# Twelve key tiles' product and denominators, and the order of GpSimd's first zero rows

## The chip, the cores and the metric

The kernel runs on one core of one Trainium2 chip. The core has five engines that run their own instruction streams and meet at semaphores: TensorE (PE in the profile; its weight loads are PEld), VectorE (DVE), ScalarE (ACT), GpSimd (POOL) and SyncE (SP), which issues the transfers. The metric is the device time in microseconds. The kernel before took 3111.95, 3116.89 and 3116.89 us in three runs; the median is 3116.89.

## The reference

Two layers of attention with a feed-forward block behind each, on x of 2 x 1024 x 1024 in fp32, each block on a layer norm of x and added to it. The attention has 32 query heads of 32 dimensions in 8 groups that share a key and value head; rotary positions; a causal softmax.

```python
q = (x @ wq).reshape(bsz, seq_len, N_HEADS, HEAD_DIM)
k = (x @ wk).reshape(bsz, seq_len, N_KV_HEADS, HEAD_DIM)
v = (x @ wv).reshape(bsz, seq_len, N_KV_HEADS, HEAD_DIM)
q = _apply_rope(q, cos, sin)
k = _apply_rope(k, cos, sin)
...
scores = jnp.einsum('bqhd,bkhd->bhqk', q, k) / np.float32(np.sqrt(HEAD_DIM))
scores = scores + mask
attn = jax.nn.softmax(scores.astype(jnp.float32), axis=-1).astype(q.dtype)
out = jnp.einsum('bhqk,bkhd->bqhd', attn, v).reshape(bsz, seq_len, N_HEADS * HEAD_DIM)
return out @ wo
```

The blocks behind are a mixing layer over four streams and a mixture of low-rank experts; the change touches neither.

## The kernel before

`build` runs attention of layer 0, the mixing layer, attention of layer 1, the output projection and the experts, one after the other. Only `attention` matters here.

**Numbers in halves.** x and the weights are split into a high part, rounded, and a low rest (`xT_hi`, `xT_lo`, `w_hi`, `w_lo`), and each projection piece is three matmuls (hi by hi, lo by hi, hi by lo; L759). Queries and keys are stacked in the same way, three parts of 32 dimensions in 96 partitions (`qst`, `kst`). Partitions 96 to 127 carry the row maximum: -1 in the keys' last row, the maximum in the queries' last row, zeros in the 31 rows between.

**Groups.** A group is one key head with its four query heads, in one batch; 2 layers x 2 batches x 8 groups make 32. For a group, the scores are computed transposed, keys in partitions, in twelve units: e counts the pairs of a query half (qc) and a key tile (ki). A unit has two steps of scores (`("ST", e, half)`, L827), which ScalarE turns into `prob` by an exponential (L560), and the steps `("PV", e, 0)`, the product with V into `ppv`, and `("PV", e, 1)`, the denominators, a product with ones, into `pden` (both L847: eight matmuls in a profile row, or two times four, each with weights 32 columns wide). Below they are called V.e and D.e. The four heads are of 512, 384, 256 or 128 columns by the unit's place at the causal edge.

**What is woven between.** The exponential wants the row maximum beforehand. So while group g is multiplied, the scores of group g+1 are computed once more in the plain direction only for their maxima: 38 uses `("S", k)` (L780) into `psh`, two banks in turn, and VectorE takes the maxima out (L647 with the causal edge, L650 without). S.k can start when VectorE has released the bank of S.(k-2) (the semaphore `sh_free`). Also into `psh` go the two projections of a later group's queries, `("P", c, i)` (eight pieces each of three matmuls); VectorE's rotation of P.0 (L635, L636, the second a shuffle) releases its bank, which is that of S.1. `("MT", 0)` transposes the maxima once VectorE has gathered them (L656); they go out to memory and back into the last row of the stacks.

**The order** is written out by `iteration()`: a dictionary `after` gives for each step what stands behind it; S uses are dealt out over the units 1 to 9 in proportion to columns. There are four orders: `body` (24 groups, all of it), `body6` (`proj=False`, 4 groups), `ahead7` (2 groups, without S and P.0, P.1, with the next batch's x tiles instead) and `body7` (2 groups, nothing woven in). Every engine walks the same list and does its own part of each step.

**The head of an attention.** VectorE takes statistics of each of the eight x tiles (`statistics`, L610), GpSimd the power -1/2 of the variance (`reciprocal_deviation`, L420), VectorE normalises (L619), TensorE transposes (L771), and projects. On GpSimd the eight powers stand first, with the first weights' low part (`w_lo`, L425) behind the sixth; then come the constant rows of the two stacks (L492, L494, L496); then the turn-over (the rotary sine part, `turn_over`, L432 and L434) of the first projection and the low part of the second weights.

Of the kernel before, what the change touches and what calls it, by code (L numbers as in the profile page):

```python
# [14 lines left out]
F32 = mybir.dt.float32  # L15
# [6 lines left out]
P = 128  # L22
B, S, D = 2, 1024, 1024
T = B * S
NT = T // P
ST_ = S // P
# [3 lines left out]
GH = 4  # L30
# [46 lines left out]
def columns(step):  # L77

    what, e, _ = step
    n = BANK - unit_offset(e)  # L80
    return 2 * max(n, BANK // 2) if what == "ST" else 4 * n


def iteration(full_s=True, proj=True, ahead=False):

    steps = [[("ST", e + 1, 0), ("ST", e + 1, 1), ("PV", e, 0), ("PV", e, 1)] for e in range(NU)]
    steps[-1] = steps[-1][2:]  # L90
    after = {step: [] for unit in steps for step in unit}
    first = []
    if proj:
        quarter = lambda c, i: [("P", c, k) for k in range(i * PIECES // 4, (i + 1) * PIECES // 4)]
        first = quarter(0, 0)
        for i, step in enumerate(steps[0][:3]):
            after[step] += quarter(0, i + 1)
        after[steps[2][1]] += [("HI", 0)]
        after[steps[3][1]] += [("LO", 0)]
        after[steps[2][0]] += [("WL", 0)]  # L100
        after[steps[4][0]] += [("WS", 0)]
        after[steps[5][0]] += [("RS", 0)]
        after[steps[10][1]] += quarter(1, 0)
        after[steps[10][2]] += quarter(1, 1) + [("RK", 0)]
        after[steps[10][3]] += quarter(1, 2) + quarter(1, 3)
    if full_s:
        window = [step for unit in steps[1:10] for step in unit]
        total, done, k = sum(map(columns, window)), 0, 0
        for step in window:
            done += columns(step)  # L110
            while k < len(USES) and k * total < done * len(USES) - total // 2:
                after[step] += [("S", k)]
                k += 1
        assert k == len(USES)
        after[steps[10][1]] += [("MT", 0)]
    after[steps[10][1]] += [("NORM", 0)]
    if ahead:


        for i in range(ST_):  # L120
            after[steps[i][0]] += [("XS", i)]
            after[steps[i][2]] += [("XN", i)]
            after[steps[i + 2][1]] += [("XT", i)]
            after[steps[i + 2][2]] += [("XC", i)] + [("XL", i + NX_AHEAD)] * (i + NX_AHEAD < ST_)
        first = [("XL", i) for i in range(NX_AHEAD)]
        for i in range(PIECES):
            after[steps[10][i * 3 // PIECES]] += [("P", "next", i)]
    order = [("ST", 0, 0), ("ST", 0, 1)] + ([("HI", 1), ("LO", 1), ("RS", 1)] if full_s else []) + first
    for unit in steps:
        for step in unit:  # L130
            order += [step] + after[step]
    return order + [("NORM", 1)]
# [57 lines left out]
def attention(nc, sem, layer, x_in, wqkv, cos_in, sin_in, swap, oT_d):  # L190
# [21 lines left out]
    ZT0, W0, SH0, R0, E0, PV0, AC0, N0, ST0, DMA0 = 4, 2, 1, 4, 2, 2, 2, 1, 2, 16  # L212

    pro, body, body6, body7 = prologue(), iteration(), iteration(proj=False), iteration(False, False)
    ahead7 = iteration(False, False, True)
    plan_pro, U_PRO = bank_plan(pro, spare=(2, 3, 4, 5))
    plan = {id(order): bank_plan(order)[0] for order in (body, body6, body7, ahead7)}
# [4 lines left out]
    with ExitStack() as ctx:  # L222
        def sb(name, shape, dt=F32):
            return ctx.enter_context(nc.sbuf_tensor(f"a{layer}_{name}", shape, dt))
# [17 lines left out]
        qst = [sb(f"qst{i}", [P, GH, S], F32R) for i in range(2)]  # L242
# [173 lines left out]
        def _(pool):  # L416
            def reciprocal_deviation(tile, k):

                pool.wait_ge(s["stats"], tile + 1)
                pool.tensor_tensor(mv[k % 2][:, 3:4], mv[k % 2][:, 2:3], nhalf[:, :], ALU.pow).then_inc(s["pow"], 1)  # L420

            def w_lo(n, par):
                pool.wait_ge(s["w_hi"], n + 1)
                pool.sem_inc(s["pool_turn"], 1)
                pool.tensor_tensor(w[par][1][:, :, :], wraw[par][:, :, :], w[par][0][:, :, :].bitcast(F32),  # L425
                                   ALU.subtract).then_inc(s["w_ready"], 1)
# [56 lines left out]
            pool.drain().then_inc(s["const"], 1)  # L483
            pool.drain().then_inc(s["w_ready"], W0)
            pool.drain().then_inc(s["roped"], R0)
            for k in range(ST_):
                reciprocal_deviation(k, k)
                if k == 5:
                    w_lo(0, 0)
            pool.drain()  # L490
            for i in range(2):
                pool.memset(kst[i][96:P, :].bitcast(F32), -1.0)  # L492
                pool.drain()
                pool.memset(kst[i][96:P - 1, :].bitcast(F32), 0.0)  # L494
                pool.drain()
                pool.memset(qst[i][96:P - 1, :, :].bitcast(F32), 0.0)  # L496
                pool.drain()
            pool.drain().then_inc(s["padded"], 1)

# [248 lines left out]
        def _(pe):  # L748
            def project(n, u, where, par, c, piece):

                _, at, prev = where
                if piece == 0:
                    pe.wait_ge(s["w_ready"], W0 + n + 1)
                    pe.wait_ge(s["sh_free"], SH0 + u + prev + 1)
                passes = [(k, a, x) for k in range(KC) for a, x in ((0, 0), (0, 1), (1, 0))]
                step = len(passes) // PIECES
                for i in range(piece * step, (piece + 1) * step):
                    k, a, x = passes[i]
                    mm = pe.matmul(bank(at), w[par][a][:, k, :], xT[x][:, k, c * BANK:(c + 1) * BANK],  # L759
                                   start=(i == 0), stop=(i == len(passes) - 1))  # L760
                if piece == PIECES - 1:
                    mm.then_inc(s["sh_ready"], 1)
# [12 lines left out]
            def row_scores(u, where, par, k):  # L775
                _, at, prev = where
                qt, kc, n, heads, _ = USES[k]
                pe.wait_ge(s["sh_free"], SH0 + u + prev + 1)
                for i, h in enumerate(heads):
                    mm = pe.matmul(psh[:, at, i * n:(i + 1) * n], qst[par][0:P - 1, h, qt * P:(qt + 1) * P],  # L780
                                   kst[par][0:P - 1, kc * BANK:kc * BANK + n], start=True, stop=True,
                                   skip_group_check=True)
                mm.then_inc(s["sh_ready"], 1)

            def transpose_max(n, u, where):
                _, at, prev = where
                pe.wait_ge(s["mx_ready"], n + 1)
                pe.wait_ge(s["sh_free"], SH0 + u + prev + 1)
                pe.transpose(psh[0:GH * ST_, at, 0:P], mx[:, 0, :], ident[:, :]).then_inc(s["sh_ready"], 1)
# [1131 lines left out]
```

## Time and profile before

| | us |
|---|---|
| runs | 3111.95, 3116.89, 3116.89 |
| profiled execution | 3121.41 |
| its span, first to last instruction | 3119.7 |
| TensorE busy in it | 2780.3 (89%) |
| VectorE busy | 1933.4 (62%) |
| ScalarE busy | 1001.4 (32%) |
| GpSimd busy | 715.2 (23%) |

The profile is one execution. Its clock column (PEclk) is the share of full speed that TensorE was granted; the mean over the span is 0.945. Three views are used: windows, which give each engine's busy time in a stretch; the timeline, which gives start, length and number of instructions of a row; and at a row's end, in brackets, how long the engine had been idle before and what released it. Matmuls overlap, so the time of one is read from start to next start, not from its length.

### The profile page before, as it was taken

The numbers are of one execution on the slowest core, as the hardware profiler recorded it, in microseconds if no ns is written. First come the engines' busy times: TensorE is split into PE (matmuls) and PEld (weight loads), VectorE is DVE, ScalarE is ACT, GpSimd is POOL, SyncE is SP. The second block draws the span as 40 slices with busy tenths as digits, with TensorE's granted clock in tenths as the row PEclk, the third lists the DMA queues.
The fourth block names the chain that finished last, engine by engine and source line by source line (L and its number), as shares of the span: only waits on it lengthen the run. The fifth ranks groups of instructions, "written<-read, shape, count | busy, mean of one in ns | idle before, by whom it ended". The sixth has DMA issues, their size and how long they took to land. (4 is left out here: it accounts for less than half of the span.)

```text
span 3119.7 us, 49191 instructions
## 1 busy us (share of the span) xinstructions
PE 2780.3 (89%) x15824; PEld 1788.4 (57%) x15824; DVE 1933.4 (62%) x4357; ACT 1001.4 (32%) x1549; POOL 715.2 (23%) x693
## 2 busy tenths in 40 slices
PE   7899998999999799652859999989999996997999
PEld 5545554655554488652646455436555542885887
DVE  4577777557777433588765677775677774324543
ACT  2143435134343411352521443433244344101000
POOL 6223231433231000000044323214223220001111
PEclk8999999999999899765979999989999998998999
DMA  3323222323131422000123323223323221443111
GB/s 139 102 64 89 70 72 72 113 73 97 56 102 30 140 81 67 0 0 0 81 115 105 101 63 89 69 64 110 94 63 97 58 77 73 158 135 148 68 67 41
DMA packets 121063, 252.84 MB, mean 81 GB/s; under 512 B 12720, under 2 KB 39728, under 8 KB 120880
## 3 DMA queue, kind: packets, MB, share of 16 engines
q1 hardware_dynamic: 120912, 251.03, 25.5%
q8 instruction: 69, 1.13, 0.2%
q14 instruction: 82, 0.67, 0.1%
HBM read 166.57 MB, written 84.41 MB: 80 GB/s over the span
## 5 line engine op out<-in xcount | busy, mean ns | idle before, releaser
L560 ACT ACTIVATE a_prob<-a_pst 128x1024 f32<-128x1024 f32 (+3 forms) x768 | 593.0, 814 | 726.2 <-PE a_pst L827 724.7
L647 DVE CUSTOM_DVE_ANT_0 a_psh<-a_psh,a_edge 128x128 f32<-128x128 f32 (+3 forms) x1024 | 487.6, 514 | 218.5 <-PE a_psh L780 208.1
L780 PE MATMUL a_psh<-a_kst,a_qst 127*128 127x512 f32 (+3 forms) x1536 | 511.7, 394 | 29.3 <-issue 12.0
L780 PEld LDWEIGHTS a_psh<-a_kst,a_qst 127*128 127x128 f32 x1536 | 255.9, 189 | 455.4 <-DVE a_mx L647 199.3
L827 PE MATMUL a_pst<-a_qst,a_kst 128*128 128x512 f32 (+2 forms) x1536 | 398.8, 361 | 28.9 <-ACT a_prob L560 11.0
L650 DVE TENSOR_REDUCE a_mx<-a_psh 128x1 f32<-128x512 f32 x512 | 343.6, 689 | 71.1 <-PE a_psh L780 65.1
L847 PE MATMUL a_ppv<-a_prob,a_vg 128*32 128x512 f32 (+3 forms) x3072 | 335.0, 508 | 15.6 <-POOL a_prob L464 10.6
L464 POOL TENSOR_SCALAR_AFFINE_SELECT a_prob<-a_prob 128x512 f32<-128x512 f32 x256 | 171.9, 672 | 759.4 <-ACT a_prob L560 758.2
L827 PEld LDWEIGHTS a_pst<-a_qst,a_kst 128*128 128x128 f32 x1536 | 267.1, 192 | 128.4 <-issue 56.2
L847 PE MATMUL a_pden<-a_prob,a_ones 128*32 128x512 f32 (+3 forms) x3072 | 332.0, 504 | 0.0
L691 DVE RECIPROCAL a_dens<-a_dens 128x512 f32<-128x512 f32 x64 | 214.6, 3353 | 75.6 <-ACT a_dens L568 66.4
L432 POOL TENSOR_TENSOR a_swp<-a_swp,a_sin 128x512 f32<-128x512 f32 x80 | 103.2, 1290 | 330.3 <-DVE a_swp L636 329.6
L759 PE MATMUL a_psh<-a_xT_hi,a_w_hi 128*128 128x512 f32 x416 | 174.4, 419 | 2.3 <-issue 1.6
L1411 PE MATMUL h_pout<-h_w,h_o 128*128 128x512 f32 x720 | 167.7, 392 | 0.8 <-DVE h_x L1288 0.8
L759 PE MATMUL a_psh<-a_xT_lo,a_w_hi 128*128 128x512 f32 x416 | 165.2, 397 | 0.0
L759 PE MATMUL a_psh<-a_xT_hi,a_w_lo 128*128 128x512 f32 x416 | 164.9, 396 | 0.0
L425 POOL TENSOR_TENSOR a_w_lo<-a_wraw,a_w_hi 128x1024 fp32r<-128x1024 f32 x50 | 119.2, 2383 | 178.9 <-ACT a_w_hi L536 163.0
L759 PE MATMUL a_pst<-a_xT_hi,a_w_hi 128*128 128x512 f32 x352 | 141.7, 403 | 13.2 <-POOL a_w_lo L425 9.0
L1411 PEld LDWEIGHTS h_pout<-h_w,h_o 128*128 128x128 f32 x720 | 134.1, 188 | 28.8 <-DMA h_wb<-in_w_branch 1.2
L647 DVE DVE_READ_ACCUMULATOR2_ANT a_mx<- 128x1 f32 x1024 | 145.0, 142 | 0.0
L759 PE MATMUL a_pst<-a_xT_lo,a_w_hi 128*128 128x512 f32 x352 | 139.5, 396 | 0.0
L759 PE MATMUL a_pst<-a_xT_hi,a_w_lo 128*128 128x512 f32 x352 | 139.1, 395 | 0.0
(217 smaller groups left out, 3958.8 us busy)
## 6 DMA issues: line engine op xcount, KB each, us to landing
a_qst<-q SPq DMA_DIRECT2D x192, 256.0 KB, 4.5
a_wraw<-in_wqkv SPq DMA_DIRECT2D x52, 512.0 KB, 5.7
q<-a_stg_hi SPq DMA_DIRECT2D x64, 256.0 KB, 2.6
q<-a_stg_lo SPq DMA_DIRECT2D x64, 256.0 KB, 2.8
oT<-a_oT SPq DMA_DIRECT2D x64, 256.0 KB, 2.5
a_kst<-kT SPq DMA_DIRECT2D x96, 128.0 KB, 3.0
h_oraw<-oT SPq DMA_DIRECT2D x16, 512.0 KB, 4.1
h_x<-in_x SPq DMA_DIRECT2D x16, 512.0 KB, 4.7
```

The source lines that it names most:

```text
L425: pool.tensor_tensor(w[par][1][:, :, :], wraw[par][:, :, :], w[par][0][:, :, :].bitcast(F32), ALU.subtract).then_inc(s["w_ready"], 1)
L432: pool.tensor_tensor(swp[c][:, :], swp[c][:, :], sin[:, c * BANK:(c + 1) * BANK], ALU.mult)
L464: pool.affine_select(out=blk, in_=blk, compare_op=ALU.is_ge, fill=0.0, base=0, pattern=[[0, GH], [1, P]], channel_multiplier=-1)\
L560: act.activation(prob[k % 2][:, 2 * half:2 * half + 2, off:], pst[:, half, :, off:], ACT.Exp, scale=scale).then_inc(s["exp_done"], 1)
L647: part = dve.tensor_tensor_reduce(scores, scores, edge[:, BANK - n:], 1.0, 2 * MASKED, ALU.add, ALU.max, mx_hq[kc][:, h, qt:qt + 1])
L650: part = dve.tensor_reduce(mx_hq[kc][:, heads[0]:heads[0] + m, qt], psh[:, at, 0:m * n].rearrange("p (m n) -> p m n", n=n), AX.X, ALU.max)
L691: dve.reciprocal(dens[:, :], dens[:, :])
L759: mm = pe.matmul(bank(at), w[par][a][:, k, :], xT[x][:, k, c * BANK:(c + 1) * BANK], start=(i == 0), stop=(i == len(passes) - 1))
L780: mm = pe.matmul(psh[:, at, i * n:(i + 1) * n], qst[par][0:P - 1, h, qt * P:(qt + 1) * P], kst[par][0:P - 1, kc * BANK:kc * BANK + n], sta ...
L827: mm = pe.matmul(pst[:, half, hh, off:], kst[par][:, ki * P:(ki + 1) * P], qst[par][:, 2 * half + hh, qc * BANK + off:(qc + 1) * BANK], st ...
L847: mm = pe.matmul(acc[h * HD:(h + 1) * HD, off:], lhs, prob[k % 2][:, h, off:], start=(ki == 0), stop=(ki == 4 * qc + 3), skip_group_check= ...
L1411: mm = pe.matmul(pout[:, half, :], o[:, par, a, k, :], w[:, b, k, half * BANK:(half + 1) * BANK], start=(i == 0), stop=(i == len(passes) - 1))
```

## The change

**The order of the groups.** In the units 0, 1, 2, 3, 9, 10 and 11 the step D.e follows V.e at once. What stood between them goes behind D.e. The S uses that the dealing would have put behind V.e of such a unit go behind the second scores step before it, so ahead of V.e. In the body order that joins V and D in the units 0, 1, 2, 9 and 10 (in 3 and 11 nothing stood between); in `body6` in 1, 2 and 9; in `ahead7` in 10 (what stood behind V.1 to V.9 there moves too, but is no work of TensorE); `body7` stays.

**The constant rows.** On GpSimd the -1 and 0 rows of the two key stacks are written ahead of the first power. The zero rows of the query stacks, one instruction of 31 x 4096 each, become four of 31 x 1024, one behind each power.

```diff
+TOGETHER = (0, 1, 2, 3, 9, 10, 11)
...
+        slot = {("PV", e, 0): ("ST", e + 1, 1) for e in TOGETHER}
         for step in window:
             done += columns(step)
             while k < len(USES) and k * total < done * len(USES) - total // 2:
-                after[step] += [("S", k)]
+                after[slot.get(step, step)] += [("S", k)]
                 k += 1
...
     order = [("ST", 0, 0), ("ST", 0, 1)] + ([("HI", 1), ("LO", 1), ("RS", 1)] if full_s else []) + first
+    for e in TOGETHER:
+        after["PV", e, 1][:0] = after["PV", e, 0]
+        after["PV", e, 0] = []
...
-            for k in range(ST_):
-                reciprocal_deviation(k, k)
-                if k == 5:
-                    w_lo(0, 0)
-            pool.drain()
             for i in range(2):
                 pool.memset(kst[i][96:P, :].bitcast(F32), -1.0)
                 pool.drain()
                 pool.memset(kst[i][96:P - 1, :].bitcast(F32), 0.0)
                 pool.drain()
-                pool.memset(qst[i][96:P - 1, :, :].bitcast(F32), 0.0)
+            for k in range(ST_):
+                reciprocal_deviation(k, k)
+                if k == 5:
+                    w_lo(0, 0)
+                pool.drain()
+                pool.memset(qst[k // GH][96:P - 1, k % GH, :].bitcast(F32), 0.0)
                 pool.drain()
             pool.drain().then_inc(s["padded"], 1)
```

TensorE in a body group, from the last matmuls of P.0 to unit 1's product. `pst` takes scores, `psh` takes P and S, REGISTER_ALU and ISA rows belong to the step behind them. Before:

```order
L759 MATMUL a_psh<-a_xT_hi,a_w_lo 128x512
L847 MATMUL a_pden<-a_prob,a_ones 32x512 x4
L825 ISA
L827 MATMUL a_pst<-a_qst,a_kst 128x256 x2
L825 REGISTER_ALU
L827 MATMUL a_pst<-a_qst,a_kst 128x256 x2
L811 REGISTER_ALU
L780 MATMUL a_psh<-a_kst,a_qst 128x128 x4
L839 REGISTER_ALU
L847 MATMUL a_ppv<-a_prob,a_vg 32x384 x4
L778 REGISTER_ALU
L780 MATMUL a_psh<-a_kst,a_qst 128x256 x2
```

After:

```order
L765 MATMUL a_psh<-a_xT_lo,a_w_hi 128x512
L765 MATMUL a_psh<-a_xT_hi,a_w_lo 128x512
L831 ISA
L833 MATMUL a_pst<-a_qst,a_kst 128x256 x2
L831 REGISTER_ALU
L833 MATMUL a_pst<-a_qst,a_kst 128x256 x2
L817 REGISTER_ALU
L786 MATMUL a_psh<-a_kst,a_qst 128x128 x4
L784 REGISTER_ALU
L786 MATMUL a_psh<-a_kst,a_qst 128x256 x2
L845 REGISTER_ALU
L853 MATMUL a_ppv<-a_prob,a_vg 32x384 x4
```

D.0 has left its place behind P.0 for one ahead of it, and S.1 (four 128 x 128 are S.0, two 128 x 256 are S.1) stands ahead of V.1 instead of behind it.

TensorE at the end of unit 8 and in unit 9 of the same group, from S.34 on. Before:

```order
L780 MATMUL a_psh<-a_kst,a_qst 128x512
L825 ISA
L827 MATMUL a_pst<-a_qst,a_kst 128x256 x2
L825 REGISTER_ALU
L827 MATMUL a_pst<-a_qst,a_kst 128x256 x2
L839 REGISTER_ALU
L847 MATMUL a_ppv<-a_prob,a_vg 32x384 x4
L778 REGISTER_ALU
L780 MATMUL a_psh<-a_kst,a_qst 128x512
L778 REGISTER_ALU
L780 MATMUL a_psh<-a_kst,a_qst 128x512
```

After:

```order
L786 MATMUL a_psh<-a_kst,a_qst 128x512
L831 ISA
L833 MATMUL a_pst<-a_qst,a_kst 128x256 x2
L831 REGISTER_ALU
L833 MATMUL a_pst<-a_qst,a_kst 128x256 x2
L784 REGISTER_ALU
L786 MATMUL a_psh<-a_kst,a_qst 128x512
L784 REGISTER_ALU
L786 MATMUL a_psh<-a_kst,a_qst 128x512
L845 REGISTER_ALU
L853 MATMUL a_ppv<-a_prob,a_vg 32x384 x4
```

S.35 and S.36, which stood behind V.9, follow the scores of unit 10 at once.

GpSimd at the head of an attention, from the first power on. Before:

```order
L420 TENSOR_TENSOR a_mv<-a_mv,a_nhalf 128x1 x6
L425 TENSOR_TENSOR a_w_lo<-a_wraw,a_w_hi 128x1024
L420 TENSOR_TENSOR a_mv<-a_mv,a_nhalf 128x1 x2
L492 MEMSET a_kst 32x1024
L494 MEMSET a_kst 31x1024
L496 MEMSET a_qst 31x4096
L492 MEMSET a_kst 32x1024
L494 MEMSET a_kst 31x1024
```

After, from the first memset to the third tile:

```order
L493 MEMSET a_kst 32x1024
L495 MEMSET a_kst 31x1024
L493 MEMSET a_kst 32x1024
L495 MEMSET a_kst 31x1024
L426 TENSOR_TENSOR a_mv<-a_mv,a_nhalf 128x1
L502 MEMSET a_qst 31x1024
L426 TENSOR_TENSOR a_mv<-a_mv,a_nhalf 128x1
L502 MEMSET a_qst 31x1024
L426 TENSOR_TENSOR a_mv<-a_mv,a_nhalf 128x1
L502 MEMSET a_qst 31x1024
```

The four rows of the key stacks are ahead of the first power, and each power has a quarter of a query stack's zero rows behind it.

## Rows read from the trace of the kernel before

**Rows 1.** Windows: stretch, length, busy of PE, PEld, DVE, ACT, POOL, PEclk, DMA share, GB/s

```profile
130.00:910.00 780.00, 748.16 (x4634) 409.22 (x4633) 543.93 (x1267) 302.91 (x425) 232.63 (x232) 0.99 0.27 80
```

**Rows 2.** Timeline, TensorE: start, length, line, operation, shapes; body, then ahead7

```profile
367.53 1.07 PE L847 MATMUL a_ppv<-a_prob,a_vg 128*32 128x512 f32 x8
369.19 1.06 PE L847 MATMUL a_pden<-a_prob,a_ones 128*32 128x512 f32 x8
...
535.52 1.07 PE L847 MATMUL a_ppv<-a_prob,a_vg 128*32 128x512 f32 x8
536.40 1.04 PE L847 MATMUL a_pden<-a_prob,a_ones 128*32 128x512 f32 x8
```

**Rows 3.** Timeline, TensorE units 0 and 1, then VectorE's shuffle of P.0

```profile
355.38 0.50 PE L759 MATMUL a_psh<-a_xT_hi,a_w_hi 128*128 128x512 f32 x1
355.71 0.40 PE L759 MATMUL a_psh<-a_xT_lo,a_w_hi 128*128 128x512 f32 x1
...
356.64 0.39 PE L759 MATMUL a_psh<-a_xT_hi,a_w_lo 128*128 128x512 f32 x1
...
357.95 0.74 PE L827 MATMUL a_pst<-a_qst,a_kst 128*128 128x256 f32 x4
358.53 0.56 PE L780 MATMUL a_psh<-a_kst,a_qst 127*128 127x128 f32 x4
359.03 0.85 PE L847 MATMUL a_ppv<-a_prob,a_vg 128*32 128x384 f32 x8
...
357.68 0.74 DVE L636 STREAM_SHUFFLE a_swp<-a_psh 128x512 f32<-128x512 f32 x1
```

**Rows 4.** Timeline, TensorE unit 2, then VectorE's last maximum for S.2

```profile
361.02 0.50 PE L780 MATMUL a_psh<-a_kst,a_qst 127*128 127x256 f32 x2
...
362.11 0.64 PE L847 MATMUL a_ppv<-a_prob,a_vg 128*32 128x256 f32 x8
362.68 0.44 PE L780 MATMUL a_psh<-a_kst,a_qst 127*128 127x384 f32 x1
...
362.06 0.47 DVE L647 CUSTOM_DVE_ANT_0 a_psh<-a_psh,a_edge 128x256 f32<-128x256 f32 x1
```

**Rows 5.** Timeline, TensorE's scores of unit 10, then VectorE on S.33, S.34

```profile
389.58 0.64 PE L827 MATMUL a_pst<-a_qst,a_kst 128*128 128x256 f32 x4
...
389.54 0.69 DVE L650 TENSOR_REDUCE a_mx<-a_psh 128x1 f32<-128x512 f32 x1 [0.37 <-PE a_psh L780]
390.15 0.69 DVE L647 CUSTOM_DVE_ANT_0 a_psh<-a_psh,a_edge 128x512 f32<-128x512 f32 x1
```

**Rows 6.** Windows: behind both idle stretches of the heads, and VectorE between the tiles

```profile
46.80:50.30 3.50, 3.45 (x8) 2.78 (x9) 0.00 (x0) 0.81 (x2) 3.36 (x3) 0.51 0.00 0
1632.50:1637.50 5.00, 5.00 (x12) 3.93 (x13) 0.00 (x0) 1.58 (x2) 4.86 (x4) 0.50 0.00 0
7.74:24.58 16.84, 8.91 (x40) 7.14 (x40) 16.10 (x33) 6.86 (x11) 7.57 (x6) 0.75 0.65 263
```

**Rows 7.** Timeline of the heads: VectorE, GpSimd, TensorE of layer 0, TensorE of layer 1

```profile
36.23 0.72 DVE L711 STREAM_SHUFFLE a_swp<-a_psh 128x512 f32<-128x512 f32 x1
...
41.81 1.28 POOL L432 TENSOR_TENSOR a_swp<-a_swp,a_sin 128x512 f32<-128x512 f32 x1 [0.37 <-issue]
...
44.46 2.34 POOL L425 TENSOR_TENSOR a_w_lo<-a_wraw,a_w_hi 128x1024 fp32r<-128x1024 f32 x1
...
46.85 0.80 PE L759 MATMUL a_pst<-a_xT_hi,a_w_hi 128*128 128x512 f32 x1 [4.06 <-POOL a_w_lo L425]
...
1632.51 0.80 PE L759 MATMUL a_pst<-a_xT_hi,a_w_hi 128*128 128x512 f32 x1 [4.92 <-POOL a_w_lo L425]
```

**Rows 8.** Timeline: GpSimd's first power, VectorE's first and last normalisation of layer 0

```profile
6.20 0.55 POOL L420 TENSOR_TENSOR a_mv<-a_mv,a_nhalf 128x1 f32<-128x1 f32 x1 [3.79 <-DVE a_mv L614]
...
7.74 0.81 DVE L619 TENSOR_SCALAR a_xin<-a_xin,a_mv 128x1024 f32<-128x1024 f32 x1
...
30.56 1.65 DVE L619 TENSOR_SCALAR a_xin<-a_xin,a_mv 128x1024 f32<-128x1024 f32 x1
```

## The prediction

> **What bounds the kernel now.** I read the windows first, then the timeline of TensorE beside that of VectorE in one typical group, then the two attention prologues. In a long window inside attention 0 TensorE is busy 748 of 780 us at a granted clock of 0.99 [rows 1]: nearly every change of its own order is paid or won one for one, unless it runs into a wait. The attention runs 32 groups of this kind, 24 of them with the full order ("body"), 53 us each. What has to be read next is therefore how long TensorE takes from one block to the next, and how near VectorE's row maxima are to being awaited. Outside the groups one more place counts: at the head of each attention TensorE stands idle for GpSimd, 4.06 us in layer 0 and 4.92 us in layer 1, and restarts at a granted clock of 0.50, the 1.2 GHz level [rows 6, 7].
>
> **What one join saves.** V is the product with V, D the denominators; both use tiles 32 columns wide, everything beside them is full width. Split by two full-width matmuls of 512 columns, V to D takes 369.19 - 367.53 = 1.66 us; adjacent, in a group whose order is already so, 536.40 - 535.52 = 0.88 [rows 2]. Two full-width matmuls in a row cost 2 x 0.2325, the rate of four from 355.71 to 356.64 [rows 3]. So 1.66 - 0.88 - 0.465 = 0.32 us go with the split; about 0.10 of it is the first full-width matmul behind a small block (355.38 to 355.71: 0.33 for 0.23 [rows 3]). D's own successor differs by 0.01 more; I take 0.33. Seven numbers stand in the table, but units 3 and 11 were adjacent already: a body group gains five joins (0, 1, 2, 9, 10), the four groups without projection three (1, 2, 9), two more groups one (10). That is 24 x 5 + 4 x 3 + 2 = 134 joins, 44 us if nothing else came to be late. The Trainium skill, "TensorEngine Tiling (Array Packing)", section Key Properties, says that changing the tiling mode drains TensorE; by that alone the sum would be the 44 us, and the rows agree with a price for each switch.
>
> **What comes to be late.** A join takes full-width matmuls out from between V and D. Where they were row-maximum scores (S), the table now puts them ahead of V, and each S needs a bank that VectorE must first have emptied. S uses two banks in turn, so S.k waits for the maximum of S.(k-2), and S.1 for the rotation of the projection P.0.
>
> *Unit 0 and 1.* From the last matmul of P.0 (356.64) to the end of VectorE's shuffle of it (357.68 + 0.74 = 358.42) pass 1.78 us [rows 3]. Today D.0, the scores of unit 2, S.0 and V.1 lie between, and S.1 comes after its bank is free. Afterwards D.0 is ahead of that last matmul and V.1 behind S.1. What is left between is 0.23 (the matmul itself), 0.48 (358.53 - 357.95 less the 0.10 of a first matmul) and 0.44 for S.0 (its 0.50 less about 0.06 for entering V): 1.15 us. TensorE starts about 0.05 after a release (362.68 against 362.06 + 0.47 and the short read behind it [rows 4]), so S.1 waits 1.83 - 1.15 = 0.68, and restarts with a first matmul of 0.33 for 0.23: 0.78.
>
> *Unit 2.* S.2 starts at 361.02; VectorE's maximum of it ends near 362.6 and S.4 starts at 362.68, 1.66 later, with V.2 in between [rows 4]. With V.2 moved behind S.4, its 362.68 - 362.11 = 0.57 and the 0.09 of entering it leave: 1.00 us of work against a shortest distance of 1.62. A wait of 0.62 and a restart of 0.10: 0.72.
>
> *Unit 9.* The scores of unit 10 start at 389.58 and would let S.35 go at 390.06; VectorE still works on S.33 until 389.54 + 0.69 = 390.23. Wait 0.22, restart 0.10. S.36 would follow 0.33 behind S.35, at 390.61, but the maximum of S.34 runs 390.15 to 390.84 and its read behind that: wait 0.30, restart 0.10 [rows 5]. Together 0.72. The transpose of the maxima (MT) hangs on S.37 and VectorE's last maximum, so it moves with them.
>
> *Unit 10.* P.1 only moves behind D.10; nothing waits for it early. Gain 0.33.
>
> Body group: 0.78 + 0.72 + 0.72 - 5 x 0.33 = +0.57. I also followed the whole group's order by hand, each step at the latest of its engine and of what it waits for: it gave 0.64 longer, since S.36 costs a little more. I take 0.62. Four body groups open a batch; their S.0 waits for the transfer of its stack anyway, so unit 0 neither gains nor loses: +0.72 + 0.72 - 4 x 0.33 = +0.12. The groups without projection: +0.72 + 0.72 - 3 x 0.33 = +0.45. The two groups with a join at unit 10 alone: -0.33, against a delay of that size because one copy of ScalarE (a_xT_hi) now stands behind two others there; 0 in sum. So 20 x 0.62 + 4 x 0.12 + 4 x 0.45 = **+14.7 us** where 44 were to be had.
>
> **The zero rows.** GpSimd writes them today after the last tile, and only then turns P's first piece over (41.81) and makes the low part of the second weights (44.46 for 2.34). TensorE waits for those until 46.85, idle 4.06 [rows 7]. Afterwards the turn-over can start when VectorE's shuffle is through, 36.23 + 0.72 = 36.95 and a latency: 37.1 for 41.81, 4.7 us sooner. The low part is then there at 44.46 + 2.34 - 4.7 = 42.1, just before TensorE wants it (46.85 - 4.06 = 42.8, less a pipeline's length). The idle 4.06 goes, and with it the slow stretch: eight matmuls at 3.45 / 8 = 0.43 instead of 0.23 [rows 6], 1.6 us. Sum 5.7. Layer 1: idle 4.92, twelve matmuls at 5.00 / 12 = 0.42, 2.2. Sum 7.1. Together 12.8.
>
> What it costs: between the tiles VectorE is the bound, busy 16.10 of 16.84 us [rows 6]. The four memsets of the key stacks, about a microsecond each, fit nearly ahead of the first power (GpSimd is idle 3.79 us there): it starts near 7.0 for 6.20 and still ends before 7.74, when tile 0 is normalised [rows 8]. But the first zero rows would be written from 7.65, just as that begins. One such meeting stands in the trace: the last tile's normalisation, 0.81 for the first, takes 1.65 at 30.56, with a memset of the key stack beside it [rows 8]. Later memsets fall a microsecond and more behind the normalisation, beside statistics. So 0.6 a layer (0 to 0.85), 1.2 in all. The Trainium skill, "SBUF — State Buffer", section SBUF: two separate sides, calls the port pair that VectorE and GpSimd share an exclusive lock, kept for a whole instruction; the row of 1.65 agrees. Net of this part: **-11.6 us**.
>
> **Sum.** +14.7 - 11.6 = +3.1. The profiled execution took 3121.4 and would take 3124.5; it lies 4.5 above the median of the runs, 3116.9, so the median becomes **3120.0**, which I forecast. Own range 3113 to 3127: 0.15 us a body group either way is 3.6, a restart that is free in one place of the four 2.4, the start 1 to 2.
>
> **Rivals.** (a) *The waits are smaller than I think* (0.14): if a pause costs only itself, without the 0.10 of a restart, four restarts in 20 groups and two in 8 give back 9.6 us: 3110. For it: I have the 0.33 of a first matmul only behind small tiles. Against: the first matmul behind the 4.06 us of idle at 46.85 is longer too, 0.80 [rows 7], though the clock has its part in that.
> (b) *The full gain* (0.06): VectorE, whose order doesn't change, starts sooner too because its banks are filled sooner, and no wait appears: 3116.9 - 44 - 12 = 3061. Against it: the distances 1.78 and 1.62 hold VectorE's own work and are not shortened by an earlier start.
> (c) *Slower: the statistics are held too* (0.10). If a memset of 0.95 beside the statistics lengthens those as it did the normalisation, each of the five tiles ahead of the first low part (done at 24.58, where the window of [rows 6] ends) loses 0.95 where VectorE has no slack: 9.5 over both layers, 3129. It decides from half that: 1.5 us lost a layer puts the run past 3123. Against it: the subtractions that VectorE makes right behind its 1.65 ran at their usual speed beside a memset.
> (d) *The gap at the head stays* (0.10): the low part at 42.1 is only 0.5 ahead of need; if ScalarE's high part or the weights' transfer are what is really late, or GpSimd is held by VectorE, a gap reopens and the clock falls again. At most 12.8 come back: 3133. The gap's releaser is GpSimd in both layers [rows 7], against it.
> The forecast's own case has 0.60. The change does what it says: the S moves stand in the order.
>
> **How the numbers follow.** A measurement of this kernel tells some 0.2%, 6.2 us, from no change: 3110.7 and 3123.1 are the bounds. Faster: (b) 0.06, half of (a) and a tail of the forecast's case, 0.18. Slower: (c) and (d) 0.20 and the quarter of the forecast's case above 3123, 0.36. Same: 0.46. The range 3106 to 3131 leaves out (b) and most of (d), with tails of the others.
>
> **What would show it.** In a body group of the profile after: V.0 to D.0 0.88 for 2.58 with six P matmuls behind it; the row of S.1 with an idle of 0.7 released by VectorE's shuffle; an idle of 0.6 ahead of S.4 released by a maximum; two short ones ahead of S.35 and S.36; group to group 53.6 for 52.95. Over the kernel the idle of the S rows that VectorE's maximum or shuffle releases grows by some 45 us. At the heads: no idle of 4 us on the low part, clock near 1.00 throughout, GpSimd's turn-over at 37 to 38, the normalisation of tile 0 at 1.4 to 1.65. Wrong would be: no idle ahead of S.1 (then (b)), idle without a slow matmul behind it (then (a)), or TensorE idle at 42 still (then (d)).

## The result, and the profile after

The kernel after takes 3123.66 us, the median of 15 runs (3118.37 to 3133.39), against 3116.89 of the kernel before (15 runs, 3111.93 to 3121.28): ratio 1.0022, 95% interval 1.0013 to 1.0032, so 4 to 10 us slower. Run again beside the experiments it gave 3124.92 against 3118.02, the same 1.0022 (1.0012 to 1.0032). The forecast was 3120.0, 3.1 us slower, with 3106 to 3131 around it: right in sign and inside the range, short by 3.7 us. The prediction counted as slower what lies above 3123.1, and gave that 0.36 against 0.46 for no change; the measured time lies just above it.

The profiled execution of after has a span of 3118.1 us, 1.6 less than that of before. The two profiles come from near the opposite ends of their kernels' spreads (the profiled execution of before took 3121.41 us, that of after 3119.78), so their spans are not to be compared; the repeated parts in them are, as will be seen.

**The start of a body group.** The timeline of after, TensorE, then VectorE, then GpSimd's mask for unit 2, for the group that starts at 347.82; it answers to [rows 3] and [rows 4]. A number in brackets at the end is the engine's idle time before the row and what released it.

```profile
347.82 1.06 PE L853 MATMUL a_ppv<-a_prob,a_vg 128*32 128x512 f32 x8
348.70 1.04 PE L853 MATMUL a_pden<-a_prob,a_ones 128*32 128x512 f32 x8
...
350.94 0.39 PE L765 MATMUL a_psh<-a_xT_hi,a_w_lo 128*128 128x512 f32 x1
351.17 0.64 PE L833 MATMUL a_pst<-a_qst,a_kst 128*128 128x256 f32 x4
351.64 0.56 PE L786 MATMUL a_psh<-a_kst,a_qst 127*128 127x128 f32 x4
352.76 0.50 PE L786 MATMUL a_psh<-a_kst,a_qst 127*128 127x256 f32 x2 [0.57 <-DVE a_swp L642]
353.19 0.85 PE L853 MATMUL a_ppv<-a_prob,a_vg 128*32 128x384 f32 x8
...
355.38 0.41 PE L833 MATMUL a_pst<-a_qst,a_kst 128*128 128x256 f32 x2
356.24 0.44 PE L786 MATMUL a_psh<-a_kst,a_qst 127*128 127x384 f32 x1 [0.46 <-DVE a_mx L653]
356.62 0.64 PE L853 MATMUL a_ppv<-a_prob,a_vg 128*32 128x256 f32 x8
...
351.98 0.72 DVE L642 STREAM_SHUFFLE a_swp<-a_psh 128x512 f32<-128x512 f32 x1
...
355.54 0.63 POOL L470 TENSOR_SCALAR_AFFINE_SELECT a_prob<-a_prob 128x512 f32<-128x512 f32 x1
```

V.0 and D.0 stand 0.88 apart, as [rows 2] had it. S.1 starts at 352.76, 1.82 behind the start of P.0's last matmul, idle 0.57, released by the shuffle; S.4 at 356.24, idle 0.46, released by a maximum. The two forecast waits are there. The rival of the full gain has fallen.

**Unit 9**, TensorE of the same group; it answers to [rows 5].

```profile
383.60 0.64 PE L833 MATMUL a_pst<-a_qst,a_kst 128*128 128x256 f32 x4
384.31 0.49 PE L786 MATMUL a_psh<-a_kst,a_qst 127*128 127x512 f32 x1
384.98 0.50 PE L786 MATMUL a_psh<-a_kst,a_qst 127*128 127x512 f32 x1 [0.17 <-DVE a_mx L653]
385.41 0.85 PE L853 MATMUL a_ppv<-a_prob,a_vg 128*32 128x384 f32 x8
```

S.35 starts 0.71 behind the first of four scores that need 0.48: 0.23 of wait, too short to be shown as idle, since a matmul's row is longer than the step to the next. S.36 follows 0.67 later instead of 0.33.

**All waits of TensorE together**, from the list of waits (total us, how often, the longest), after:

```profile
PE a_psh L786 <- DVE a_mx L653: 25.5, 81, 0.8
...
PE a_psh L786 <- DVE a_swp L642: 11.2, 20, 0.6
```

and before:

```profile
PE a_psh L780 <- DVE a_mx L647: 8.4, 29, 0.5
```

The S rows wait 36.7 us where it was 8.4; the 20 waits on a shuffle are exactly those of the body groups that open no batch. The forecast had this idle grow by some 45 us, and the list shows 28. It shows too little: from start to start S.1 waits 352.76 - 351.64 - 0.44 (the work of S.0) = 0.68 where 0.57 stands in the brackets, S.4 0.62 for 0.46, and S.35 0.23 for nothing.

**The heads.** Windows of after where before stood idle; they answer to [rows 6].

```profile
42.00:50.00 8.00, 8.00 (x37) 6.62 (x36) 2.70 (x6) 1.58 (x2) 5.68 (x6) 1.00 0.00 0
1628.00:1638.00 10.00, 10.00 (x45) 8.26 (x45) 2.71 (x6) 1.58 (x2) 7.69 (x7) 1.00 0.16 61
```

TensorE is busy throughout at a granted clock of 1.00; both idle stretches of [rows 7] are gone with the half-clock matmuls behind them. The timeline has the cost, and GpSimd's new start:

```profile
7.76 1.47 DVE L625 TENSOR_SCALAR a_xin<-a_xin,a_mv 128x1024 f32<-128x1024 f32 x1
...
12.77 1.27 DVE L616 BATCH_NORM_STATS2 a_stat<-a_prob 128x6 f32<-128x512 f32 x2
...
25.35 1.54 DVE L625 TENSOR_SCALAR a_prob<-a_prob,a_mv 128x1024 f32<-128x1024 f32 x1
...
7.74 0.95 POOL L502 MEMSET a_qst<- 31x1024 f32 x1
...
12.19 0.95 POOL L502 MEMSET a_qst<- 31x1024 f32 x1
...
25.40 0.95 POOL L502 MEMSET a_qst<- 31x1024 f32 x1
...
36.93 1.30 POOL L438 TENSOR_TENSOR a_swp<-a_swp,a_sin 128x512 f32<-128x512 f32 x1 [4.92 <-DVE a_swp L717]
...
39.62 2.39 POOL L431 TENSOR_TENSOR a_w_lo<-a_wraw,a_w_hi 128x1024 fp32r<-128x1024 f32 x1
```

The turn-over starts at 36.93 (forecast 37.1), the low part is there at 42.0 (42.1). The first normalisation takes 1.47 for the 0.81 of [rows 8], +0.66 (forecast 0.6), and a second one, at 25.35, takes 1.54. Both end 0.54 behind the end of the memset beside them (9.23 against 8.69, 26.89 against 26.35), although one starts 0.02 behind its memset and the other 0.05 ahead of it. The Trainium skill, "SBUF — State Buffer", section SBUF: two separate sides, has the shared port pair as a lock kept for a whole instruction by whoever starts first; the memset at 7.74, 0.02 ahead of the normalisation, takes its usual 0.95 and the normalisation 0.66 more, which agrees. The row at 25.35 agrees only if the normalisation takes the lock later than its row starts; how much later is worked out at the end.

**The two groups of the `ahead7` order.** Here the change moved no work of TensorE except at unit 10, and the forecast counted 0. In after, ScalarE's copy of an x tile (a_xT_hi), which stood behind V.3, stands behind D.3 and so behind the two copies that empty `ppv` and `pden`; TensorE's transposes of the next x tile wait for the subtraction behind it:

```profile
518.38 0.43 PE L853 MATMUL a_ppv<-a_prob,a_vg 128*32 128x128 f32 x8
...
519.09 0.59 ACT L573 COPY a_pvs<-a_ppv 128x512 f32<-128x512 f32 x1 [0.56 <-PE a_pden L853]
519.57 0.59 ACT L574 COPY a_dens<-a_pden 128x512 f32<-128x512 f32 x1
...
520.05 1.10 ACT L548 ACTIVATE a_xT_hi<-a_psh 128x512 fp32r<-128x512 f32 x2
...
521.53 1.16 PE L777 MATMUL a_psh<-a_ident,a_vT 128*128 128x128 f32 x8 [1.39 <-DVE a_xT_lo L632]
...
522.63 1.06 PE L853 MATMUL a_ppv<-a_prob,a_vg 128*32 128x512 f32 x8
```

V.3 to V.4 takes 4.25 in both groups, for 3.21 and 3.48 before. In the first of them the copy starts 1.67 behind V.3, for 0.64 before. The join at unit 10 gives 0.02 to 0.04 here, not 0.33.

### The profile page after: what moved, and what is told of

Its sections match the earlier page's. It is cut to its first block and busy times, and to the rows that moved or that the text cites. A ratio compares the mean times of both kernels' runs of the same rounds, so it can differ in the third digit from the quotient of the medians.

```text
span 3118.1 us, 49229 instructions
## 1 busy us (share of the span) xinstructions
PE 2755.7 (88%) x15824; PEld 1803.0 (58%) x15824; DVE 1927.1 (62%) x4357; ACT 1001.1 (32%) x1549; POOL 714.0 (23%) x705
## 5 line engine op out<-in xcount | busy, mean ns | idle before, releaser
L786 PE MATMUL a_psh<-a_kst,a_qst 127*128 127x512 f32 (+3 forms) x1536 | 518.6, 396 | 57.4 <-DVE a_mx L653 25.5
L833 PE MATMUL a_pst<-a_qst,a_kst 128*128 128x512 f32 (+2 forms) x1536 | 396.2, 359 | 29.7 <-ACT a_prob L566 11.9
L833 PEld LDWEIGHTS a_pst<-a_qst,a_kst 128*128 128x128 f32 x1536 | 269.4, 193 | 109.0 <-issue 34.8
L853 PEld LDWEIGHTS a_pden<-a_prob,a_ones 128*32 128x32 f32 x3072 | 85.7, 111 | 113.3 <-issue 102.3
```

What stands on the lines that cost most here:

```text
L833: mm = pe.matmul(pst[:, half, hh, off:], kst[par][:, ki * P:(ki + 1) * P], qst[par][:, 2 * half + hh, qc * BANK + off:(qc + 1) * BANK], st ...
L853: mm = pe.matmul(acc[h * HD:(h + 1) * HD, off:], lhs, prob[k % 2][:, h, off:], start=(ki == 0), stop=(ki == 4 * qc + 3), skip_group_check= ...
```

## The experiments

The quoted text in front of each measurement was on record before that run. The runs were made in three batches, each with the kernel before beside it: the ratios are to its medians, 3118.02 for the first four experiments (the two parts, the kernel after again, joins at 0 and 10), 3116.82 for joins at 2, at 9, at 1 and 10 and the first version with P.0 early, 3119.10 for the other three. What repeats best between executions is the distance of one group's V.0 from the next: taken from the starts in the timeline, the 20 body groups that don't open a batch sum to 1055.4 and 1055.2 us in two kernels with the old order (before, and the zero rows alone), to 1067.1, 1066.7 and 1066.7 in three executions with the new one. Everything else, the transfers at a batch's start and the half-clock stretches above all, moves a total by some 5 us either way, so the medians are given with their intervals, and the theories are judged by rows.

### The two parts apart

The zero rows alone: the kernel before with this edit.

```diff
-            for k in range(ST_):
-                reciprocal_deviation(k, k)
...
-                pool.memset(qst[i][96:P - 1, :, :].bitcast(F32), 0.0)
+            for k in range(ST_):
+                reciprocal_deviation(k, k)
+                if k == 5:
+                    w_lo(0, 0)
+                pool.drain()
+                pool.memset(qst[k // GH][96:P - 1, k % GH, :].bitcast(F32), 0.0)
+                pool.drain()
```

> The kernel before with the new order of GpSimd's constant rows alone; no join. Theory (waits): the idle of 4.06 and 4.92 us on the low part goes and the slow clock behind it too, tile 0's normalisation takes 1.47 instead of 0.81; body groups stay 52.97 us apart; 11 to 13 us faster than before, ratio 0.996. Rival (the gap stays, or something later gives it back): ratio within 0.999 to 1.001.

Measured: 3104.78 against 3118.02, ratio 0.9954 (0.9939 to 0.9969), body groups 52.95; no idle on the low part is left in either layer, and tile 0's normalisation takes 1.48. The joins alone, the kernel before with the whole table and GpSimd as it was:

```diff
+TOGETHER = (0, 1, 2, 3, 9, 10, 11)
...
-                after[step] += [("S", k)]
+                after[slot.get(step, step)] += [("S", k)]
...
+    for e in TOGETHER:
+        after["PV", e, 1][:0] = after["PV", e, 0]
+        after["PV", e, 0] = []
```

> The kernel before with all seven numbers of TOGETHER, GpSimd as before. Theory (waits): body groups 53.5 apart instead of 52.97, the heads idle 4.06 and 4.92 as before; 14 to 18 us slower, ratio 1.005. Rival (joins are worth something and the slower result comes from the heads): at most 3 us slower, ratio under 1.001.

Measured: 3135.68, ratio 1.0050 (1.0038 to 1.0062), body groups 53.5. TensorE stood idle 4.24 and 5.04 us for the low part, where before had 4.06 and 4.92. And the kernel after once more:

> The kernel after unchanged, on the same chip as the other three. Theory: the two parts add up, so its ratio is that of the zero rows alone times that of the joins alone: 0.996 x 1.005 = 1.001, body groups 53.5. Rival (they meet somewhere): it lies 5 us or more off that product.

Measured: 1.0022 (1.0012 to 1.0032). The product of the parts is 0.9954 x 1.0050 = 1.0004, with an interval of about 0.0019 either way (the root of the sum of the squares of the two half-widths, 0.0015 and 0.0012). 1.0022 lies 0.0018 above it, 5.6 us: by the mark that was set, 5 us, this is the rival's case, but it is within the interval, so neither is shown. Each part works as forecast, one gains 14 us, the other costs 16; whether they meet at a third place these runs don't settle, and no wait in the traces points to one.

### One place at a time

Unit 2 alone, `TOGETHER = (2,)` in the kernel after:

> The kernel after with TOGETHER = (2,): S.4 ahead of V.2 and nothing else moved. Theory (waits): an idle of about 0.6 ahead of S.4 released by VectorE's maximum, then D.2 joined: V.2 to V.3 0.5 shorter, V.1 to V.2 0.7 to 0.9 longer, body groups 53.3 to 53.4. Rival (S.4's wait in the kernel after is only what the shift by S.1 left over): no idle ahead of S.4, body groups 52.6.

Measured: body groups 53.33, V.1 to V.2 3.99 for 3.08, V.2 to V.3 2.74 for 3.25, and the idle:

```profile
355.56 0.44 PE L786 MATMUL a_psh<-a_kst,a_qst 127*128 127x384 f32 x1 [0.46 <-DVE a_mx L653]
```

Unit 9 alone, `TOGETHER = (9,)`:

> The kernel after with TOGETHER = (9,): S.35 and S.36 ahead of V.9, nothing else moved. Theory (waits): idle ahead of S.35 of 0.2 and ahead of S.36 of 0.3, both released by VectorE; V.8 to V.9 1.24 longer as in the kernel after (the two S now stand in it), V.9 to V.10 0.86 shorter, body groups 53.35. Rival (the row maxima have slack here): no idle, body groups 52.6.

Measured: body groups 53.36, V.8 to V.9 5.03 for 3.79, V.9 to V.10 4.03 for 4.89, and

```profile
381.05 0.49 PE L786 MATMUL a_psh<-a_kst,a_qst 127*128 127x512 f32 x1 [0.16 <-DVE a_mx L653]
```

Each of the two joins costs a body group more than it gives: +0.36 and +0.39 net. Each was run once, 3116.58 and 3112.14 us, which alone decides nothing; the verdict rests on the rows.

### Joins that wait for no bank

`TOGETHER = (0, 10)` in the kernel after, units whose join puts no S ahead of V:

> The kernel after with TOGETHER = (0, 10): the two units whose join puts no row-maximum score ahead of V. Theory (waits): no idle ahead of S.1 beyond today's, body groups 52.97 - 0.66 = 52.3, 26 joins of unit 10 and 24 of unit 0 at 0.33 are 16.5 us, with the heads' 12 together 28 us faster than before, ratio 0.991. Rival (a join is not worth 0.33 where the engines behind set the pace): body groups stay 52.9 to 53.0 and the ratio is that of the zero rows alone, 0.996.

Measured: 3114.5, ratio 0.9991 (0.9980 to 1.0003), body groups 53.3. This is neither the theory's 52.3 nor the rival's 52.95, and my theory of banks alone falls. V.0 to V.1 is 4.31 for 4.65 and V.10 to V.11 5.31 for 5.72, both joins won; but V.1 to V.2 is 4.13 for 3.08. TensorE, then GpSimd, in the group that starts at 347.29:

```profile
355.73 0.64 PE L853 MATMUL a_ppv<-a_prob,a_vg 128*32 128x256 f32 x8 [0.98 <-POOL a_prob L470]
...
352.38 1.28 POOL L438 TENSOR_TENSOR a_swp<-a_swp,a_sin 128x512 f32<-128x512 f32 x1 [4.05 <-DVE a_swp L642]
353.80 1.28 POOL L440 TENSOR_TENSOR a_rot<-a_rot,a_swp 128x512 f32<-128x512 f32 x1
355.03 1.23 POOL L470 TENSOR_SCALAR_AFFINE_SELECT a_prob<-a_prob 128x512 f32<-128x512 f32 x2
```

V.2 works on a tile at the causal edge and needs GpSimd's mask. GpSimd keeps the written order: the turn-over of P.0, two rows that take 2.65 us up to the mask's start, then that mask (the last row holds it and the next unit's). Whoever puts D.0 ahead of P.0's last pieces delays the shuffle, the turn-over, the mask and V.2, one behind the other. In the kernel before there is next to no room for it, as GpSimd's row there shows:

```profile
361.26 0.64 POOL L464 TENSOR_SCALAR_AFFINE_SELECT a_prob<-a_prob 128x512 f32<-128x512 f32 x1
```

It ends at 361.90, and V.2 starts at 362.11 [rows 4].

Three runs test this second theory. First `TOGETHER = (1, 10)`, which leaves P.0 alone and brings V.2 nearer to the mask:

> The kernel after with TOGETHER = (1, 10): P.0 stays where it was, S.1 ahead of V.1. Theory (mask behind the turn-over): in the runs with unit 0 joined, V.2 waited for GpSimd's causal mask, which stands on its queue behind the 2.7 us turn-over of P.0; in the kernel before that mask ends at 361.90 and V.2 starts at 362.11. So V.2 can come only 0.15 to 0.2 sooner: body groups 52.97 - 0.40 - 0.17 = 52.4, 13.7 us and the heads' 12 faster than before, ratio 0.992. Rival (only VectorE's banks bound it): no wait at V.2, body groups 52.97 - 0.73 = 52.25, ratio 0.990.

Measured: 3090.49, ratio 0.9920 (0.9904 to 0.9937), body groups 52.41, where the bank theory would have had 52.25. No idle is shown at V.2, but the rows tell the wait: GpSimd's mask, then V.2 of one group.

```profile
349.86 0.64 POOL L470 TENSOR_SCALAR_AFFINE_SELECT a_prob<-a_prob 128x512 f32<-128x512 f32 x1
...
350.55 0.64 PE L853 MATMUL a_ppv<-a_prob,a_vg 128*32 128x256 f32 x8
```

V.2 starts 0.05 behind the mask's end, here and in the like groups of the trace (0.05 to 0.06 in 16), for 0.20 to 0.22 before. Next `TOGETHER = (0, 1)`:

> The kernel after with TOGETHER = (0, 1). Theory (mask behind the turn-over): S.1 waits 0.57 for VectorE's shuffle as in the kernel after, and V.2, which no longer has S.4 ahead of it, waits some 0.4 to 0.5 more for GpSimd's mask, which ends 8.35 after V.0; V.0 to V.2 8.4 where it was 7.73, body groups 53.6, longer than with all joins (53.54). Rival (only VectorE's banks bound it): no wait at V.2, V.0 to V.2 7.9, body groups 53.1.

Measured: body groups 53.67, V.0 to V.2 5.37 + 3.04 = 8.41, a single run of 3117.16 us, and both waits, the second for the mask:

```profile
352.62 0.50 PE L786 MATMUL a_psh<-a_kst,a_qst 127*128 127x256 f32 x2 [0.56 <-DVE a_swp L642]
...
356.09 0.64 PE L853 MATMUL a_ppv<-a_prob,a_vg 128*32 128x256 f32 x8 [0.46 <-POOL a_prob L470]
```

Two joins cost more here than all of them (53.54): in the kernel after, the wait ahead of S.4 covers the mask's. Last, P.0 early, with joins at 0, 1 and 10:

```diff
-TOGETHER = (0, 1, 2, 3, 9, 10, 11)
+TOGETHER = (0, 1, 10)
...
-        for i, step in enumerate(steps[0][:3]):
+        for i, step in enumerate((steps[0][0], steps[0][1], steps[0][1])):
             after[step] += quarter(0, i + 1)
```

> The kernel after with TOGETHER = (0, 1, 10) and the last two pieces of P.0 ahead of V.0 instead of behind D.0, so that VectorE's rotation and GpSimd's turn-over start 1.9 us sooner. Theory: S.1 waits for neither and V.2's mask is not late; three joins are won in full, body groups 52.97 - 0.33 - 0.33 - 0.40 = 51.9, 25 us and the heads' 12 faster than before, ratio 0.988. Rival (a wait for something else, the exponential or the banks, comes up in units 0 to 2 as soon as the two are gone): body groups 52.3 or more.

Measured: 3084.39, ratio 0.9896 (0.9880 to 0.9913), body groups 51.93; no row of TensorE in units 0 to 2 has an idle of its own. With P.0 early and the whole table:

> The kernel after, all joins, with the last two pieces of P.0 ahead of V.0. Theory: the wait ahead of S.1 and its restart go (0.6 to 0.8), those ahead of S.4, S.35 and S.36 stay: body groups 52.97 - 1.39 (joins 0, 1 and 10 and their entries, as the run with the three alone had 51.93) + 0.36 (unit 2) + 0.39 (unit 9) = 52.7; with the heads 3098 to 3100, ratio 0.994. Rival (the waits of unit 2 and 9 stem from P.0 too): 52.0 or less, ratio under 0.991.

Measured: body groups 52.75, S.4's wait unchanged:

```profile
353.84 0.44 PE L786 MATMUL a_psh<-a_kst,a_qst 127*128 127x384 f32 x1 [0.47 <-DVE a_mx L653]
```

The groups are as forecast, but the time is not: 3108.38, ratio 0.9959 (0.9943 to 0.9974), 8 us and more above what I had written. That sum was short: the 20 groups are 1045.5 for 1029.4 of the run before, 16.1, and the eight other groups that have units 2 and 9 add 0.72 + 0.72 - 0.66 = 0.78 each, 6.2; from 3084.39 that is 3106.7. The two `ahead7` groups, whose V.3 to V.4 is at 4.25 again, give 1.6 more from V.2 to V.11 (35.26 and 35.30 for 34.72 and 34.26): 3108.3. The two medians come from different batches, so the agreement to 0.1 us is partly luck.

### The meeting of memset and normalisation

The version with P.0 early, zero rows behind the powers 2, 3, 4, 6 and 7 only:

```diff
+ZERO_AT = {2: (0,), 3: (1,), 4: (2,), 6: (3,), 7: (4, 5, 6, 7)}
...
-                pool.memset(qst[k // GH][96:P - 1, k % GH, :].bitcast(F32), 0.0)
-                pool.drain()
+                for h in ZERO_AT.get(k, ()):
+                    pool.memset(qst[h // GH][96:P - 1, h % GH, :].bitcast(F32), 0.0)
+                    pool.drain()
```

> The version with P.0 early and joins at 0, 1, 10, and GpSimd's zero rows behind powers 2, 3, 4, 6 and four behind the last, none behind 0, 1 and 5. Theory (a memset that runs as a normalisation starts holds it): tile 0 is normalised in 0.81 instead of 1.47 and everything up to TensorE's first projection comes 0.66 sooner in both layers, 1.3 us in all, ratio 0.989. Rival (the 1.47 has another cause): it stays at 1.4 or more.

Measured: 3079.85, ratio 0.9865 (0.9841 to 0.9888), and the first normalisation is short again:

```profile
7.82 0.80 DVE L627 TENSOR_SCALAR a_xin<-a_xin,a_mv 128x1024 f32<-128x1024 f32 x1
```

Its ratio and that of the version without this edit overlap (0.9880 to 0.9913), so 1.3 us of gain are not shown by the time, only the 0.66 by the row. Nor does the gain reach TensorE in layer 0, whose first projection behind the tiles starts at 36.90 with this edit, and at 36.90 and 37.76 in the two versions with P.0 early without it. Of all kernels run it is the fastest, 39 us ahead of the 3119.10 of before beside it.

## Why the prediction was right, and where it was off

**What a join saves.** Right where nothing waits: 4.65 - 4.31 = 0.34 at unit 0 for the forecast 0.33; at unit 10 5.72 - 5.31 = 0.41, a little more.

**S.1's wait.** Right. Forecast 0.68 and a restart, 0.78; measured 0.57 of idle, and two matmuls of 256 columns that take 353.19 - 352.76 = 0.43 to V where 0.24 of work and about 0.09 for entering V would be expected: the restart's 0.10 is there. In the run with joins at 1 and 10, where S.1 waits for nothing, S.0 and S.1 together take 347.90 - 347.13 = 0.77 up to V.1, so S.1 0.33. That also answers the rival of smaller waits, which lived on the restart being free.

**S.4's wait.** Right: it starts 0.86 behind the scores' row at 355.38, which need 0.24, so 0.62 as forecast (shown as 0.46 idle). From V.0 to V.3 the kernel after took 5.38 + 3.42 + 2.74 = 11.54 for 4.65 + 3.08 + 3.25 = 10.98, +0.56, where the steps gave 0.78 + 0.72 - 0.99 = +0.51.

**Unit 9 and 10.** Forecast 0.72 - 0.66 = +0.06; measured 5.03 + 4.03 + 5.35 for 3.79 + 4.89 + 5.72, +0.01. A body group in all +0.57, as the hand sum had it (the forecast took 0.62): 20 groups 11.3 to 11.9 more where 12.4 stood.

**The heads.** Forecast -11.6; the zero rows alone measured -13 by medians. The idle and the clock went as worked out. One more half-clock stretch of before, later in layer 0, is gone in the profile of after, which was in no sum. It stands at 87 to 91 us in the joins alone as well, but in the repeat of after a like one is back at 83 to 86 (a clock of 0.56), so the new order doesn't remove it for certain. Its window in before:

```profile
87.80:91.20 3.40, 3.38 (x9) 2.90 (x10) 2.35 (x9) 0.00 (x0) 0.00 (x0) 0.51 0.99 224
```

A second normalisation met a memset (1.54 at 25.35), which the forecast had excluded: the low part of the first weights delays that memset until the normalisation starts. The last one (31.63) took 0.93. On the other side the 1.65 of before at the last tile, which the forecast quoted as a price, is gone, and it had not counted this as a gain. What counts is when the last normalisation ends: 32.56 for 32.21 in layer 0; in layer 1, from the start of tile 0's, 24.68 for 23.40. That is 0.35 and 1.28, 1.6 in all for a forecast 1.2: near, with two errors that cancelled in part. The rival of held statistics fell: the statistics beside the memset at 12.19 took their 1.27.

**The 3.7 us that are missing.** One term was mis-sized in the direction of the miss: the 0 for the two `ahead7` groups. The forecast named the delay, a copy of ScalarE behind two others, and set it equal to the gain of the join; from V.2 to V.11 these groups take 35.3 to 35.9 in the four profiles with all joins at hand (after, its repeat, the joins alone, P.0 early with all joins) for 34.2 to 34.8 in before and the zero rows alone, 0.9 more each, 1.9 in all. The groups without projection cost 0.51 each (0.29 + 0.34 - 0.51 + 1.24 - 0.85) for a forecast 0.45. With the 11.5 of the body groups (for 12.4) that makes 15.4 us; what the four that open a batch do is hidden under their transfers. The joins alone measured 1.0050, 15.7 us (17.7 by medians), for a forecast 14.7, the zero rows alone 13 to 14 for 11.6, and both together +6.8 for +3.1. Each term is within its interval, but the +3.1 is just below that of the whole (4 to 10 us); the sum of the two measured terms is +1 to +4, and so is that of the rows, 15.4 less the 13 of the heads. The errors found work against each other: 1.9 us too little in the `ahead7` groups, 0.9 too much in the body groups, 1.5 to 2.5 too little gain at the heads. What makes +6.8 of +1 to +4 shows in no row, and the cause stays open, as said under the two parts.

**What the forecast did not see.** The step on unit 0 priced one consequence of a later P.0, VectorE's bank, and stopped there: this step of the working was incomplete. The same shuffle also starts GpSimd's turn-over, and the mask of unit 2 is queued behind that. It didn't show in the result, because in the kernel after the waits ahead of S.1 and S.4 hold V.2 back by more than the mask does: V.2 starts at 356.62, the mask ends at 355.54 + 0.63 = 356.17. The number was right while one of the reasons was not there; the first version built on the reasons, joins at 0 and 10, missed by 25 us. That the missing reason did no harm to the forecast was luck. It would have been found by following GpSimd's queue behind the turn-over, not only the engine that releases the bank.

## What to carry to other kernels

Adjacent small-tile blocks save a fixed price for each switch, but only if what stood between them has somewhere to go; ask for each piece moved whether the engine that must free its place is ahead by as much as the work taken out. Follow a delayed step through every queue behind it, not only to the first consumer: here a projection that came one block of 0.9 us later was paid for at a bank of VectorE, and where that was not in the way, at a mask of GpSimd. Where one early producer feeds several chains, moving it ahead of the whole block (P.0 before V.0) opens all of them at once, and was worth more than any single join: with all joins in place a body group went from 53.54 to 52.75. A group of the order that looks untouched needs the same reading: two of them cost 1.9 us here because a copy changed places on ScalarE.

## What the hardware showed that I had not expected

- A memset and a VectorE normalisation (128 x 1024, 0.81 alone) that meet: the normalisation ends 0.54 or 0.55 us behind the memset's end, whether it started 0.57 behind the memset's start (and took 0.93), 0.02 behind it (1.47) or 0.05 and 0.15 ahead of it (1.54, and the 1.65 of [rows 8]). All 64 such meetings in twelve of the thirteen traces fit. So what it waits for it asks for about 0.81 - 0.55 = 0.26 behind the start of its row, an estimate from these rows, and it holds it for the last 0.55. The other way round the memset waits: in layer 1 of before one starts at 1616.39, while a normalisation runs until 1616.82, and takes 1.32 for 0.95. Statistics of 1.27 and subtractions of two half tiles at 1.28 run beside the same memset at their own speed.
- A wait of 0.23 us of TensorE is not shown as idle, and longer ones are shown 0.1 to 0.2 too short: they are seen only from start to start.
- The 20 body groups repeat to 0.05% (1067.1 and 1066.7 in after and its repeat), while the times of one kernel differ by 5 us and more. The four groups that open a batch take 219 to 233 us over all traces, and the stretches at half the clock come and go.
